# A decoder layer on one core: feed-forward product formed by DVE from the up bank, WKV denominators inverted in pairs, ACT's copy of the up bank dropped, and another order in every queue

## The chip, the cores and the metric

One Trainium2 chip, one of its cores. The metric is the device time of the kernel in microseconds; lower is better. Engines are called as in the profile: PE (TensorE), DVE (VectorE), ACT (ScalarE), POOL (GpSimd), SP (SyncE, which here only issues DMAs).

## What is computed

One decoder layer on 16 sequences of 128 tokens with 256 channels, in float32. First comes an attention over the 16 heads of one token (not over tokens), with a rotary turn, then a WKV recurrence along the 128 tokens, then a feed-forward block whose activations and weights are quantised:

```python
def attn(x):                      # per token: 16 heads of 16
    q, k, v = rope(x @ wq.T), rope(x @ wk.T), x @ wv.T
    w = softmax(einsum('bshd,bstd->bsht', q, k) / sqrt(16))
    return einsum('bsht,bstd->bshd', w, v) @ wo.T
def wkv_step(aa, bb, pp, kt, vt): # along the tokens, per channel
    ww = u + kt; q = max(pp, ww); e1 = exp(pp - q); e2 = exp(ww - q)
    y = (e1 * aa + e2 * vt) / (e1 * bb + e2)
    ...                           # aa, bb decay by exp(-exp(time_decay))
def ffn(x):                       # 256 -> 704 -> 256, weights to -1, 0, 1
    h = silu(bitlinear(x, w1)) * bitlinear(x, w2)
    return bitlinear(h, w3)
x = layernorm(x + attn(x))
x = layernorm(x + wkv(k=x, v=ctx))
x = layernorm(x + ffn(x))
```

`bitlinear` scales each token's activations by 127 over their largest absolute value, rounds them, and multiplies by weights rounded to -1, 0 or 1 by the mean of their absolute values.

## The kernel before

A tile is one sequence: 128 tokens by 256 channels, `TILES` = 16. The kernel is a software pipeline written out by hand, without a scheduler. Each engine has its own in-order queue. Each queue is written by a function `step(at)` that `run_steps` (L75) calls for `s` = 0 to 21; `on(at(d), stage)` issues `stage` for tile `s - d`, if there is one. So the list in an engine's `step` is at once its order within a step and the distance between the tiles that it serves: `at(0)` is the youngest tile, `at(6)` the oldest. `once(at(d), ...)` issues a piece for tile 0 alone. The engines are tied together only by semaphores, and each stage names the counts that it waits for, both for its inputs and for the buffers that it overwrites.

The stages of a tile, in the order of the data:

- Attention. PE `project_q`, `project_kv` (L382 to L394), fp32, into the bank `ps_qkv`; DVE `copy_q` and ACT `copy_kv` put them into `qkv_tok`; DVE turns them with 32x32 block transposes (`q_to_dmajor`, `k_to_dmajor`, `turn_v`); PE `block_v` turns v, ACT `copy_v_blocks` copies it. PE `score` (64 small products), DVE `max_quads`, `max_rows`, `max_hi_part`, `max_lo_part` find the row maxima, PE `shift` subtracts them in the banks, ACT `exp_scores` takes the exponentials of two banks. PE `weigh_v` in two halves, DVE `heads_to_tokens`, `recip_sums`, `normalise`; PE `turn_attn`, ACT `copy_attn`, PE `project_out`, DVE `residual(.,0)`.
- Each of the three layernorms: DVE `moments`, `mean_var`; POOL `inv_std` (three small operations); ACT `layernorm`.
- WKV. PE `turn_k`, ACT `exp_k` (four exponentials into `past` and `now`), POOL `weigh_past`, `weigh_now`, DVE `scan` (L930), POOL `add_now` (L715) makes `frac`, which holds the denominators `frac[:, 0]` and the numerators `frac[:, 1]` of all 256 channels; DVE `recip_den` (L938) inverts the denominators, POOL `divide` (L725) multiplies; PE `turn_y`, DVE `residual(.,1)`.
- Feed-forward. DVE `amax_of_x`, `floor_x`, `recip_x`, ACT `scale_x`, POOL `whole_x`, PE `turn_xq`, ACT `copy_xq`. Then twice, for halves of 352 columns: PE `up` (L502) writes the gate half into bank `ps_a` and the up half into bank `ps_b`; ACT `tanh_gate`; DVE `gate_up` (L961); ACT `copy_up` (L625) copies `ps_b` to `up_s`; POOL `hidden` (L741) multiplies. DVE `amax_of_h`, `floor_h`, `recip_h`, `scale_of_h`, ACT `scale_h`, POOL `whole_h`, PE `turn_hq`, ACT `copy_hq`, PE `down`, DVE `residual(.,2)`, the last layernorm and SP `store`.

POOL has no part in anything that lies in PSUM: whatever it multiplies has been copied to SBUF. Once per launch the weights are rounded: DVE `weight_sums` (L1005), PE `sum_weights`, DVE `weight_scales`, ACT `round_weights` (L646), DVE `cut_weights`, POOL `ternary_weights` (L772). These are long instructions, and they stand in the queues of the first steps.

The waits that the change touches read before:

```python
# PE up(k, half)
wait(pe, up_copied[1], k.t)          # half 0
wait(pe, gate_done[0], k.t + 1)      # half 1
wait(pe, up_copied[0], k.t + 1)
# POOL hidden(k, half)
wait(pool, up_copied[half], k.t + 1)
wait(pool, gate_done[half], k.t + 1)
wait(pool, h_scaled, k.t)
```

## Time and profile before

| | us |
|---|---|
| three runs | 263.08, 262.02, 260.38 |
| median | 262.02 |
| profiled execution | 262.2 |
| its span, first to last instruction | 260.4 |
| PE busy | 208.2 (80%) |
| DVE busy | 217.7 (84%) |
| ACT busy | 160.9 (62%) |
| POOL busy | 161.5 (62%) |

The profile is of one execution. The span is what its rows cover; 1.8 us of the time lie around it. The core has three phases: a fill to about 57 us in which the pipeline is not full and the weights are prepared, a steady stretch to about 201 us, and a tail in which it runs empty. Times in the timeline count from the span's start. An instruction's duration there and the distance to the next start differ a little, since the end of one overlaps the start of the next.

### The profile page before, as it was taken

How to read it: one execution, taken by the hardware profiler on the slowest of the kernel's cores; microseconds unless marked ns; L12 is line 12 of the kernel's file. 1: busy time of each engine (PE TensorE's matmuls, PEld its weight loads, DVE VectorE, ACT ScalarE, POOL GpSimd, SP SyncE). 2: the span in 40 equal slices, each digit the busy share in tenths (PEclk: the TensorE clock that was granted, in tenths of full speed). 3: DMA queues.
4: the chain of work that ended last, by engine and by line, in shares of the span. 5: the costliest groups of instructions: out<-in, count | busy, mean ns of one | idle time of the engine just before them, and what ended most of it. 6: DMA issues, size and time to landing. Idle time of an engine off the chain costs nothing.

```text
span 260.4 us, 9989 instructions
## 1 busy us (share of the span) xinstructions
PE 208.2 (80%) x3778; PEld 139.9 (54%) x3778; DVE 217.7 (84%) x544; ACT 160.9 (62%) x329; POOL 161.5 (62%) x336
## 2 busy tenths in 40 slices
PE   1759699989899999999999999999997795625611
PEld 0235457657666666666666666766665662413310
DVE  2534987999999999999999999999999977686331
ACT  2212175446686877777777787777777665655631
POOL 0100007647866869696968778787777787876541
PEclk9986869999999999999999999999999757555665
DMA  6920002102020020212201120203020201000001
GB/s 194 369 66 23 3 1 65 58 7 64 4 64 3 3 83 23 65 29 58 61 26 43 44 71 17 84 3 83 5 63 3 63 3 40 10 13 21 0 20 42
DMA packets 11968, 12.34 MB, mean 47 GB/s; under 512 B 1872, under 2 KB 11152, under 8 KB 11920
## 3 DMA queue, kind: packets, MB, share of 16 engines
q1 hardware_dynamic: 11200, 11.67, 14.5%
q8 instruction: 30, 0.49, 0.8%
q14 instruction: 18, 0.15, 0.2%
q10 hardware_dynamic: 720, 0.03, 0.2%
HBM read 9.60 MB, written 2.10 MB: 45 GB/s over the span
## 4 chain that ended last, share of the span: by engine, by line
PE 50%; DVE 22%; issue 18%; ACT 4%; POOL 3%; DMA 1%; DVEq 1%; POOLq 0%; ACTq 0%
PE ps_qkv L393 13%; PE ps_s L429 9%; PE ps_o L476 5%; PE ps_w L379 4%; DVE amax_h L972 4%; PE ps_c L528 4%; DVE vT L863 3%; PE ps_a L514 3%; DVE qkD L858 3%; PE ps_b L514 3%; DVE gate L965 2%; DVE den_rec L941 2%; PE ps_o L379 2%; DVE wsum L1009 2%; PE ps_o L462 2%
## 5 line engine op out<-in xcount | busy, mean ns | idle before, releaser
L393 PE MATMUL ps_qkv<-wqkv,xT 128*128 128x512 f32 x64 | 35.5, 683 | 1.9 <-DVE qkv_tok L842 1.9
L733 POOL TENSOR_TENSOR var_eps<-mv,eps 128x1 f32<-128x1 f32 x48 | 9.2, 192 | 39.8 <-DVE mv L925 39.3
L745 POOL TENSOR_TENSOR hid<-gate,up_s 128x352 f32<-128x352 f32 x32 | 29.8, 932 | 2.1 <-ACT up_s L628 1.8
L736 POOL TENSOR_TENSOR rstd<-var_eps,minus_half 128x1 f32<-128x1 f32 x48 | 26.4, 551 | 3.8
L941 DVE RECIPROCAL den_rec<-frac 128x256 f32<-128x256 f32 x16 | 27.7, 1733 | 0.0
L429 PE MATMUL ps_s<-qkD 20*64 20x64 f32 x1024 | 23.9, 234 | 3.3 <-PE ps_s L429 3.3
L462 PE MATMUL ps_o<-probs,v_blk 64*32 64x64 f32 x1024 | 21.7, 225 | 4.6 <-DVE res L908 3.6
L577 ACT ACTIVATE qkv_tok<-ps_qkv 128x512 f32<-128x512 f32 x16 | 9.6, 598 | 25.3 <-PE ps_qkv L393 25.3
L387 PE MATMUL ps_qkv<-wqkv,xT 128*128 128x256 f32 x64 | 19.8, 431 | 6.1 <-DMA wqkv<-wqkv_in 5.3
L429 PEld LDWEIGHTS ps_s<-qkD 20*64 20x64 f32 x1024 | 19.8, 143 | 8.1 <-PE ps_s L429 5.1
L660 ACT ACTIVATE hqT<-ps_c 128x768 bf16<-128x768 bf16 x16 | 13.0, 811 | 16.4 <-PE ps_c L521 16.4
L462 PEld LDWEIGHTS ps_o<-probs,v_blk 64*32 64x32 f32 x1024 | 16.4, 110 | 12.0 <-DVE res L908 6.2
L588 ACT ACTIVATE probs<-ps_s 128x512 f32<-128x512 f32 x32 | 17.8, 599 | 7.8 <-PE ps_s L444 7.7
L644 ACT ACTIVATE x<-res,nmr,rstd 128x256 f32<-128x256 f32 x32 | 19.1, 597 | 4.9 <-POOL nmr L738 1.9
L869 DVE TRANSPOSE_TENSOR_REDUCE quad_max<-ps_s 128x32 f32<-128x1024 f32 x16 | 19.8, 1236 | 1.9 <-PE ps_s L429 1.9
L965 DVE SCALAR_TENSOR_TENSOR gate<-th,ps_a 128x352 f32<-128x352 f32 x32 | 16.0, 499 | 6.3 <-ACT th L623 6.2
L444 PEld LDWEIGHTS ps_s<-neg_eye,max_hi 128*64 128x64 bf16 x512 | 17.7, 115 | 6.6 <-issue 5.4
L623 ACT ACTIVATE th<-ps_a,half_gate 128x352 f32<-128x352 f32 x32 | 17.5, 548 | 5.6 <-PE ps_b L514 4.9
L721 POOL TENSOR_TENSOR frac<-state,now 128x512 f32<-128x512 f32 x16 | 19.0, 1185 | 1.5 <-DVE state L935 1.5
L935 DVE TENSOR_TENSOR_SCAN state<-w_tab,past 128x516 f32<-128x516 f32 x16 | 19.7, 1233 | 0.0
L920 DVE BATCH_NORM_STATS2 stats<-res 128x6 f32<-128x256 f32 x48 | 19.4, 405 | 0.2
L444 PE MATMUL ps_s<-neg_eye,max_hi 128*64 128x64 bf16 x512 | 19.5, 200 | 0.1
(110 smaller groups left out, 569.5 us busy)
## 6 DMA issues: line engine op xcount, KB each, us to landing
xT<-xT_in SPq DMA_DIRECT2D x16, 128.0 KB, 2.4
x_res<-x_in SPq DMA_DIRECT2D x16, 128.0 KB, 2.7
ctxT<-ctxT_in SPq DMA_DIRECT2D x16, 128.0 KB, 2.4
out<-y_out SPq DMA_DIRECT2D x16, 128.0 KB, 1.7
w_raw<-w_in SPq DMA_DIRECT2D x2, 704.0 KB, 6.7
wqkv<-wqkv_in SPq DMA_DIRECT2D x2, 384.0 KB, 4.2
w_raw<-w_in SPq DMA_DIRECT2D x1, 640.0 KB, 8.6
wo<-wo_in SPq DMA_DIRECT2D x1, 256.0 KB, 4.9
```

Source lines behind the costliest of these rows:

```text
L387: last = mm(ps_q, xT[k.slot][:, h, :], wqkv[:, h, 0:C], start=h == 0, stop=h == 1)
L393: last = mm(ps_kv, xT[k.slot][:, h, :], wqkv[:, h, C:3 * C], start=h == 0, stop=h == 1)
L429: last = mm(ps_s[64 * half:64 * half + 64, g % 2, col:col + BLK], kk, q, start=(g < 2 and b < 2), stop=False, skip_group_check=True)
L444: last = mm(o, m, neg_eye[:, half, :], start=False, stop=part is max_lo, skip_group_check=True)
L462: last = mm(ps_o[PAD * g:PAD * g + PAD, dst:dst + BLK], v_blk[k.slot][rows, jj, g, :], probs[rows, g % 2, src:src + BLK], start=True, stop ...
L736: g.tensor_tensor(rstd[i][:], var_eps[i][:], minus_half[:], ALU.pow).then_inc(rstd_done[i], 1)
L745: g.tensor_tensor(hid[:, half * FH:(half + 1) * FH], gate[half][:], up_s[half][:], ALU.mult).then_inc(hid_done[half], 1)
L869: v.tensor_reduce(quad_max[:].rearrange("p s c -> p (s c)"), ps_s[:].rearrange("p b (c x) -> p (b c) x", x=PAD), AX.X, ALU.max, apply_tran ...
L920: v.bn_stats(stats[i][:], res[i][:]).then_inc(stats_done[i], 1)
L935: v.tensor_tensor_scan(flat(state), flat(w_tab), flat(past), 0.0, ALU.mult, ALU.add).then_inc(scanned, 1)
L941: v.reciprocal(den_rec[:], frac[:, 0]).then_inc(den_recips, 1)
L965: v.scalar_tensor_tensor(gate[half][:], th[half][:], 1.0, ps_a[:, 0:FH], ALU.add, ALU.mult).then_inc(gate_done[half], 1)
```

## The change

The reciprocals are taken in pairs: for two neighbouring tokens with denominators a and b, the kernel inverts a x b and multiplies each numerator by the other denominator and by that one reciprocal. POOL forms the pair products (`pair_dens`) and the cross products (`cross_terms`) and, in `divide`, multiplies by the reciprocal, which is read twice by a step of 0. DVE's `recip_den` then has 128x128 elements instead of 128x256. `U_CUT`, the bound on the exponents' offsets, goes from 60 to 50, so that a product of two denominators stays in range. The feed-forward product `hidden` moves from POOL to DVE and reads `ps_b` in PSUM itself; ACT's `copy_up` and the buffers `up_s` are gone. All queues are written in another order, with other distances between the tiles.

```diff
-U_CUT = 60.0
+U_CUT = 50.0
...
-        den_rec = sb("den_rec", [P, HALVES, P])
+        den_pair = sb("den_pair", [P, HALVES, P // 2])
+        cross = sb("cross", [P, HALVES, P])
+        den_rec = sb("den_rec", [P, HALVES, P // 2])
...
             def up(k, half):
...
-                    wait(pe, up_copied[1], k.t)
+                    wait(pe, hid_done[1], k.t)
                 else:
                     wait(pe, gate_done[0], k.t + 1)
-                    wait(pe, up_copied[0], k.t + 1)
+                    wait(pe, hid_done[0], k.t + 1)
...
-            def copy_up(k, half):
-                wait(act, up_done[half], k.t + 1)
-                wait(act, hid_done[half], k.t)
-                fn(up_s[half][:], ps_b[:, 0:FH], ACT.Copy).then_inc(up_copied[half], 1)
...
             def add_now(k):
...
-                wait(pool, den_recips, k.t)
-                wait(pool, y_ready, k.t)
+                wait(pool, pairs_done, k.t)
+                wait(pool, crossed, k.t)
...
+            even, odd = slice(0, P, 2), slice(1, P, 2)
+            def pair_dens(k):
+                wait(pool, frac_done, k.t + 1)
+                wait(pool, den_recips, k.t)
+                g.tensor_tensor(den_pair[:], frac[:, 0, :, even], frac[:, 0, :, odd], ALU.mult).then_inc(pairs_done, 1)
+            def cross_terms(k):
+                wait(pool, frac_done, k.t + 1)
+                wait(pool, y_ready, k.t)
+                g.tensor_tensor(cross[:, :, even], frac[:, 1, :, even], frac[:, 0, :, odd], ALU.mult)
+                g.tensor_tensor(cross[:, :, odd], frac[:, 1, :, odd], frac[:, 0, :, even], ALU.mult).then_inc(crossed, 1)
             def divide(k):
-                wait(pool, frac_done, k.t + 1)
+                wait(pool, crossed, k.t + 1)
                 wait(pool, den_recips, k.t + 1)
                 wait(pool, y_turned, k.t)
-                g.tensor_tensor(yT[:], frac[:, 1], den_rec[:], ALU.mult).then_inc(y_ready, 1)
+                g.tensor_tensor(yT[:].rearrange("p h (n l) -> p (h n) l", l=2),
+                                cross[:].rearrange("p h (n l) -> p (h n) l", l=2),
+                                den_rec[:].rearrange("p h n -> p (h n)").unsqueeze(2).broadcast_to([P, C // 2, 2]),
+                                ALU.mult).then_inc(y_ready, 1)
...
-            def hidden(k, half):                        # on POOL
-                wait(pool, up_copied[half], k.t + 1)
-                wait(pool, gate_done[half], k.t + 1)
-                wait(pool, h_scaled, k.t)
-                g.tensor_tensor(hid[:, half * FH:(half + 1) * FH], gate[half][:], up_s[half][:], ALU.mult
-                                ).then_inc(hid_done[half], 1)
...
             def recip_den(k):
-                wait(dve, frac_done, k.t + 1)
+                wait(dve, pairs_done, k.t + 1)
                 wait(dve, y_ready, k.t)
-                v.reciprocal(den_rec[:], frac[:, 0]).then_inc(den_recips, 1)
+                v.reciprocal(den_rec[:], den_pair[:]).then_inc(den_recips, 1)
...
+            def hidden(k, half):                        # on DVE
+                wait(dve, gate_done[half], k.t + 1)
+                wait(dve, h_scaled, k.t)
+                v.tensor_tensor(hid[:, half * FH:(half + 1) * FH], gate[half][:], ps_b[:, 0:FH], ALU.mult
+                                ).then_inc(hid_done[half], 1)
```

The lists in the five `step` functions are new as a whole. SP issues `load_x`, `load_ctx`, `store` and the feed-forward weights, in this order, as `at(1)`, `at(0)`, `at(5)` and once `at(1)`, where it had the store at 6, the weights at 0, x at 0 and the context at 1. PE's step now begins with `block_v` and `project_out` and ends with `down`; DVE's begins with `residual(.,0)` and ends with `residual(.,2)`, `hidden(.,1)`. For example, of DVE:

```diff
-                on(at(1), max_quads)
+                on(at(0), max_quads)
-                on(at(3), scan)
+                on(at(2), scan)
-                on(at(6), residual, 2)
+                on(at(5), residual, 2)
```

DVE in the steady stretch, from `scale_of_h` (L989, s_h) on. The names are `mv` and `stats` for the layernorms, `den_rec` the reciprocal, `qkD` and `o_tok` transposes, `gate` the product of tanh and gate bank. Before:

```order
L989 TENSOR_SCALAR s_h<-rec_h,s_h 128x1
L925 BN_AGGR mv<-stats 128x2
L941 RECIPROCAL den_rec<-frac 128x256
L858 STREAM_TRANSPOSE qkD<-qkv_tok 128x16x16x2
L965 SCALAR_TENSOR_TENSOR gate<-th,ps_a 128x352
L920 BN_STATS stats<-res 128x6
L890 STREAM_TRANSPOSE o_tok<-ps_o 128x512
L925 BN_AGGR mv<-stats 128x2
L911 TENSOR_TENSOR res<-ps_w,x_0 128x256
L895 RECIPROCAL o_rec<-o_tok 128x16
L920 BN_STATS stats<-res 128x6
L996 TENSOR_SCALAR s_out<-c_h,k_down 128x1
```

The same engine after, also from `scale_of_h` (now L1001); `hid` is the feed-forward product:

```order
L1001 TENSOR_SCALAR s_h<-rec_h,s_h 128x1
L925 BN_STATS stats<-res 128x6
L868 STREAM_TRANSPOSE vT<-qkv_tok 128x16x16x2
L930 BN_AGGR mv<-stats 128x2
L895 STREAM_TRANSPOSE o_tok<-ps_o 128x512
L970 SCALAR_TENSOR_TENSOR gate<-th,ps_a 128x352
L900 RECIPROCAL o_rec<-o_tok 128x16
L977 TENSOR_TENSOR hid<-gate,ps_b 128x352
L905 TENSOR_TENSOR attn<-o_tok,o_rec 128x256
L874 TENSOR_REDUCE quad_max<-ps_s 128x32
L1008 TENSOR_SCALAR s_out<-c_h,k_down 128x1
L881 TENSOR_REDUCE row_max<-quad_max 128x16
```

The reciprocal of the denominators now stands further ahead in the step, the first gate product is followed two places later by `hid`, and the second gate product is the next row behind those shown.

DVE in the fill, around the weight sums (`wsum`) and scales (`wmean`, `wrec`, `k_gate`). Before:

```order
L863 STREAM_TRANSPOSE vT<-qkv_tok 128x16x16x2
L858 STREAM_TRANSPOSE qkD<-qkv_tok 128x16x16x2
L1009 TENSOR_REDUCE wsum<-w_raw 128x1 x3
L890 STREAM_TRANSPOSE o_tok<-ps_o 128x512
L1019 TENSOR_SCALAR wmean<-ps_a 128x3
L1022 RECIPROCAL wrec<-wmean 128x3
L1024 TENSOR_SCALAR k_gate<-wmean 128x1
```

DVE in the fill, after:

```order
L913 TENSOR_TENSOR res<-ps_o,x_res 128x256
L925 BN_STATS stats<-res 128x6
L847 TENSOR_TENSOR qkv_tok<-ps_qkv,turn_gain 128x16x16
L930 BN_AGGR mv<-stats 128x2
L1021 TENSOR_REDUCE wsum<-w_raw 128x1 x3
L858 STREAM_TRANSPOSE qkD<-qkv_tok 128x16x16x2
L863 STREAM_TRANSPOSE qkD<-qkv_tok 128x16x16x2
```

The sums moved behind tile 0's first residual and tile 2's `copy_q`, and the scales to the end of that step. On ACT the rounding (`w_raw`) moved accordingly; before it stood between `copy_v_blocks` and `copy_attn` (`attnT`):

```order
L583 ACTIVATE v_blk<-ps_qkv 128x512
L650 ACTIVATE w_raw<-w_raw,magic,wrec 128x2x704 x2
L650 ACTIVATE w_raw<-w_raw,magic,wrec 128x1536
L593 ACTIVATE attnT<-ps_o 128x256
L577 ACTIVATE qkv_tok<-ps_qkv 128x32x16
```

ACT after, at the same place of the preparation:

```order
L585 ACTIVATE v_blk<-ps_qkv 128x512
L647 ACTIVATE w_raw<-w_raw,magic,wrec 128x2x704 x2
L647 ACTIVATE w_raw<-w_raw,magic,wrec 128x1536
L590 ACTIVATE probs<-ps_s 128x512 x2
L579 ACTIVATE qkv_tok<-ps_qkv 128x32x16
```

It now stands ahead of the exponentials (`probs`) of tile 2 and of `copy_kv` (`qkv_tok`) of tile 3.

## Rows read from the trace of the kernel before

**Rows 1.** The page, chain that ended last, share of the span by engine.
```profile
PE 50%; DVE 22%; issue 18%; ACT 4%; POOL 3%; DMA 1%; DVEq 1%; POOLq 0%; ACTq 0%
```

**Rows 2.** Busy time by stretch; last columns are PE's granted clock, DMA share, GB/s.
```profile
142.66:155.02 12.36, 11.58 (x237) 8.13 (x237) 12.33 (x34) 9.53 (x20) 9.63 (x21) 1.00 0.19 56
...
204.80:217.00 12.20, 10.06 (x157) 7.28 (x157) 8.98 (x22) 8.40 (x18) 9.69 (x20) 0.58 0.09 27
...
229.00:241.00 12.00, 5.58 (x24) 2.92 (x24) 9.34 (x22) 6.27 (x11) 8.26 (x18) 0.50 0.04 12
```

**Rows 3.** Groups of instructions by shape: busy us, mean ns, idle before, releasers.
```profile
L745 POOL TENSOR_TENSOR hid<-gate,up_s 128x352 f32<-128x352 f32 x32 | 29.8, 932 | 2.1 <-ACT up_s L628 1.8 <-DVE gate L965 0.2
L941 DVE RECIPROCAL den_rec<-frac 128x256 f32<-128x256 f32 x16 | 27.7, 1733 | 0.0
...
L721 POOL TENSOR_TENSOR frac<-state,now 128x512 f32<-128x512 f32 x16 | 19.0, 1185 | 1.5 <-DVE state L935 1.5
...
L965 DVE SCALAR_TENSOR_TENSOR gate<-th,ps_a 128x352 f32<-128x352 f32 x32 | 16.0, 499 | 6.3 <-ACT th L623 6.2
...
L713 POOL TENSOR_TENSOR now<-now,ctxT 128x256 f32<-128x256 f32 x16 | 11.6, 728 | 0.0
...
L900 DVE TENSOR_TENSOR attn<-o_tok,o_rec 128x256 f32<-128x256 f32 x16 | 7.6, 475 | 0.1
...
L908 DVE TENSOR_TENSOR res<-ps_o,x_res 128x256 f32<-128x256 f32 x16 | 6.5, 404 | 0.0
...
L895 DVE RECIPROCAL o_rec<-o_tok 128x16 f32<-128x16 f32 x16 | 3.9, 241 | 0.0
```

**Rows 4.** Timeline of DVE in a steady step: start us, us, what.
```profile
146.54 1.73 DVE L941 RECIPROCAL den_rec<-frac 128x256 f32<-128x256 f32 x1
148.19 0.65 DVE L858 STREAM_TRANSPOSE qkD<-qkv_tok 128x512 f32<-128x512 f32 x1
148.77 0.48 DVE L965 SCALAR_TENSOR_TENSOR gate<-th,ps_a 128x352 f32<-128x352 f32 x1
149.17 0.41 DVE L920 BATCH_NORM_STATS2 stats<-res 128x6 f32<-128x256 f32 x1
```

**Rows 5.** Timeline of ACT in the same step.
```profile
146.55 0.97 ACT L655 ACTIVATE hq<-hid,magic,s_h 128x704 f32<-128x704 f32 x1
147.43 0.54 ACT L623 ACTIVATE th<-ps_a,half_gate 128x352 f32<-128x352 f32 x1
147.87 0.45 ACT L628 ACTIVATE up_s<-ps_b 128x352 f32<-128x352 f32 x1
149.36 0.81 ACT L660 ACTIVATE hqT<-ps_c 128x768 bf16<-128x768 bf16 x1 [1.04 <-PE ps_c L521]
150.07 0.59 ACT L644 ACTIVATE x<-res,nmr,rstd 128x256 f32<-128x256 f32 x1
150.57 0.56 ACT L623 ACTIVATE th<-ps_a,half_gate 128x352 f32<-128x352 f32 x1
...
152.14 0.61 ACT L604 ACTIVATE past<-ps_w,u_past 128x128 f32<-128x128 f32 x2
152.64 0.62 ACT L604 ACTIVATE now<-ps_w,u_now 128x128 f32<-128x128 f32 x2
```

**Rows 6.** Timeline of DVE in the fill.
```profile
26.00 4.76 DVE L1009 TENSOR_REDUCE wsum<-w_raw 128x1 f32<-128x1408 f32 x3
...
43.03 1.37 DVE L900 TENSOR_TENSOR attn<-o_tok,o_rec 128x256 f32<-128x256 f32 x1
...
54.31 0.39 DVE L842 TENSOR_TENSOR qkv_tok<-ps_qkv,turn_gain 128x256 f32<-128x256 f32 x1
```

**Rows 7.** Timeline of ACT in the fill.
```profile
31.85 4.57 ACT L650 ACTIVATE w_raw<-w_raw,magic,wrec 128x1408 f32<-128x1408 f32 x3 [5.02 <-DVE k_gate L1024]
```

**Rows 8.** Timeline of DVE in the tail.
```profile
219.36 0.41 DVE L908 TENSOR_TENSOR res<-ps_o,x_res 128x256 f32<-128x256 f32 x1
...
248.39 0.89 DVE L972 TENSOR_REDUCE amax_h<-hid 128x1 f32<-128x704 f32 x1 [0.15 <-POOL hid L745]
```

More of the change, by code:

```diff
@@ L185, in decoder_layer @@
         gate = [sb(f"gate{i}", [P, FH]) for i in range(2)]
-        up_s = [sb(f"up_s{i}", [P, FH]) for i in range(2)]
         hid = sb("hid", [P, HIDDEN])
@@ L301, in decoder_layer @@
         gate_done = [sem(f"gate_done{i}") for i in range(2)]
-        up_copied = [sem(f"up_copied{i}") for i in range(2)]
         hid_done = [sem(f"hid_done{i}") for i in range(2)]
@@ L1026, in step @@
             def step(at):
-                once(at(0), wkv_tables)
-                on(at(4), mean_var, 1)
+                on(at(2), residual, 0)
+                on(at(4), amax_of_x)
+                on(at(2), moments, 0)
                 on(at(0), copy_q)
-                on(at(5), gate_up, 1)
-                on(at(0), q_to_dmajor)
-                on(at(6), residual, 2)
-                on(at(1), max_quads)
-                once(at(2), cut_weights, 0)
-                on(at(4), amax_of_x)
@@ L1036, in step @@
-                on(at(1), max_rows)
-                on(at(4), floor_x)
-                once(at(2), cut_weights, 1)
-                on(at(1), max_hi_part)
-                on(at(4), recip_x)
-                once(at(2), cut_weights, 2)
-                on(at(1), max_lo_part)
-                on(at(3), scan)
-                on(at(0), turn_v)
-                on(at(5), amax_of_h)
-                on(at(2), residual, 0)
-                on(at(5), floor_h)
-                on(at(5), recip_h)
-                on(at(2), moments, 0)
@@ L1050, in step @@
-                on(at(5), scale_of_h)
-                on(at(2), mean_var, 0)
-                on(at(3), recip_den)
-                on(at(0), k_to_dmajor)
-                once(at(1), weight_sums)
-                on(at(4), gate_up, 0)
-                on(at(6), moments, 2)
-                on(at(1), heads_to_tokens)
-                once(at(1), weight_scales)
-                on(at(6), mean_var, 2)
-                on(at(3), residual, 1)
+                on(at(4), floor_x)
+                on(at(3), recip_den)
@@ new lines, in step @@
+                on(at(4), recip_x)
+                on(at(6), moments, 2)
+                once(at(3), cut_weights, 0)
+                on(at(2), mean_var, 0)
+                once(at(2), weight_sums)
+                on(at(5), amax_of_h)
+                once(at(3), cut_weights, 1)
+                on(at(6), mean_var, 2)
+                on(at(5), floor_h)
+                on(at(0), q_to_dmajor)
+                once(at(3), cut_weights, 2)
+                on(at(0), k_to_dmajor)
+                on(at(3), residual, 1)
@@ L1061, in step @@
+                on(at(5), recip_h)
+                on(at(5), scale_of_h)
+                on(at(3), moments, 1)
+                on(at(0), turn_v)
+                on(at(3), mean_var, 1)
+                on(at(1), heads_to_tokens)
+                on(at(4), gate_up, 0)
                 on(at(1), recip_sums)
-                on(at(3), moments, 1)
+                on(at(4), hidden, 0)
+                on(at(1), normalise)
+                on(at(0), max_quads)
                 on(at(5), scale_of_out)
-                on(at(1), normalise)
+                on(at(0), max_rows)
@@ L1066, in _ @@
+                on(at(4), gate_up, 1)
+                on(at(0), max_hi_part)
+                on(at(2), scan)
+                on(at(0), max_lo_part)
+                once(at(2), weight_scales)
+                on(at(5), residual, 2)
+                on(at(4), hidden, 1)
+                once(at(1), wkv_tables)
             run_steps(step)
```

76 lines of the change are left out of this document (38 added, 38 removed).

## The prediction

> **What bounds the kernel now.** Read first the chain that ended last, by engine: PE has half of it and DVE 22%, so neither alone is the answer [rows 1]. Then the busy time by stretch. In the steady stretch one tile passes every 12.36 us; DVE is busy 12.33 us of it and PE 11.58, ACT 9.53, POOL 9.63 [rows 2]. DVE never rests there, so the period is DVE's work; the chain runs through PE only where PE happens to feed DVE in time. In the tail (from about 201 us) DVE is busy 8.98 us of 12.20 and PE's granted clock is 0.58, then 0.50, which is the 1.2 GHz level [rows 2]: there the time is the latency of the last tile's chain. So three questions: what is DVE's work per tile after the change, does the new order keep DVE fed, and what become of fill and tail.
>
> **DVE's work per tile.** The page's durations overlap a little, so I price by the distance from one start to the next. The reciprocal of 128x256 takes 1733 ns, that of 128x16 241 ns [rows 3]: (1733-241)/240 = 6.2 ns per column, so 128x128 is 241 + 112 x 6.2 = 0.94 us, 0.80 less. By distance it is 1.65 us now (146.54 to 148.19) [rows 4] and 0.85 after. Added are two products of 128x352 with one operand in PSUM. No such row exists; the nearest are the gate operation of the same width and also with one operand in PSUM, 499 ns (0.40 by distance, 148.77 to 149.17), and the residual add of 128x256, 404 ns [rows 3, 4]. At the row of its own width one costs 0.41, two 0.82. A product cheaper than the narrower residual add is excluded, dearer than the gate by a tenth is the other end: 0.31 to 0.45, so -0.18 to +0.10 per tile. `recip_h` and `scale_of_h` now stand side by side and the second waits for the first, but `floor_h` and `recip_h` no longer do; that cancels within 0.03. Sum: 12.36 - 0.80 + 0.82 + 0.02 = 12.40 us. The two headline edits cancel on the engine that bounds.
>
> **What the other engines get.** ACT loses two copies of 0.45 us (147.87 is one of them) [rows 5], about 0.9 per tile. POOL loses two products of 932 ns, 1.86 [rows 3], and gains three of 128x128. POOL's two-input rows of 128x512 and 128x256 are 1185 and 728 ns [rows 3], 1.79 ns per column, so 0.50 each by the line and 0.73 at most if the step of two elements costs as much as twice the columns: 1.5 to 2.2. Neither engine bounds; this is worth nothing unless it feeds DVE. On PE, `up(.,1)` waited for the copy of ACT and the gate product; it now waits for gate and then `hidden` on DVE, 0.5 us later. PE has 0.78 us per tile to spare, so that is hidden in the steady stretch, and paid in the tail, twice per tile. In return hidden goes straight to `amax_of_h` on the same engine in 0.5 instead of 0.93 plus a handoff.
>
> **Does the new order keep DVE fed?** I laid the new DVE step out by distances from `residual(.,0)` = 0. The tightest place is from `scale_of_h` (5.42) to the second gate operation (9.84): 4.42 us of DVE work. ACT must do beside it, without a gap, `scale_h` 0.88, tanh 0.44, a layernorm 0.50, the four exponentials 1.00, `copy_hq` 0.71 and the second tanh to its end 0.55, with 0.30 of handoffs: 4.38 us [rows 5]. Slack 0.04. Also tight: `copy_q` to `project_kv` to `copy_kv` to `k_to_dmajor` (3.1 of 3.4 us) and the first gate, 0.0. Everything else has 0.3 or more, `scan` among them (it starts at 10.35, `weigh_now` ends at 10.0). Ready in time, so 12.40, with up to 0.3 more per tile where a handoff is a little longer than I count.
>
> POOL and DVE in each other's way is a cost this trace shows: `normalise`, 475 ns on average [rows 3], took 1.37 us at 43.03 [rows 6], while POOL rounded weights. The Trainium skill, SBUF — State Buffer (Who interferes with whom), says that a DVE instruction with two SBUF inputs and a GpSimd one that reads SBUF exclude each other, the second to issue waiting for all of the first, and that with one SBUF input DVE is not touched; the row agrees. By that page the new `hidden`, which reads PSUM and one SBUF operand, costs nobody anything.
>
> **Fill.** The weight sums hold DVE 4.76 us at 26.00 [rows 6] and PE waits behind them. Now they stand one step later, after `copy_q` of tile 2, where `project_kv` covers some of them. But the rounding, 4.57 us of ACT at 31.85 [rows 7], now stands ahead of both exponentials of tile 2 and `copy_kv` of tile 3. Walking the new order through with the durations of this trace (handoffs 0.05): sums at 31.5 to 36.2, maxima of tile 2 at 42.8, rounding 43.3 to 47.8, `copy_kv` of tile 3 ends 49.4 though its projection stood at 47.3, POOL casts the weights 47.6 to 51.9, which holds the past terms of tile 1 until 53.8, DVE ends step 3 at 55.6. Copy_q of tile 4 is then at 55.6 + 0.94 = 56.5, against 54.31 [rows 6]; but by then the new DVE order has taken also tile 3's row maxima, 1.5 us, which the old had before it. So the fill is worth 0.7 us the wrong way, with 2 us of doubt on either side.
>
> **Steady.** Step 4 lacks the operations of the tiles 5 and 6 behind: 12.40 - 1.69 - 0.43 = 10.28; step 5 is 11.97; steps 6 to 15 are 10 x 12.40 = 124.0. DVE's step 16 starts at 55.6 + 146.25 = 201.9.
>
> **Tail.** Now `residual(15,0)` is at 219.36 and the last `amax_of_h` at 248.39 [rows 8], 12.0 us before the end of the span. Walked with PE at the slow level, the new steps 16 to 19 come to 12.8 (heads of tile 15 wait for a slow `weigh_v`), 12.5, 11.2 and 9.6 us, 46.1 in all: `amax_of_h` of tile 15 at 248.0. `residual(15,0)` comes at 214.7, 4.7 us sooner than before, but this is given back: the new order puts `scan` and `residual(.,2)` between the second gate and `hidden(.,1)`, and `amax_of_x` only behind the whole of the next step, so layernorm 1 of tile 15 is read 7 us after its residual. From there the old 12.0 us stand: amax to `scale_h`, turn, `down`, layernorm, store, of which nothing was changed. Span 260.0.
>
> **Sum.** 260.0 + 1.8 (the profiled execution took 262.2 for a span of 260.4) = 261.8 us. The median of the runs shown is 262.02, so this is no change that can be told: about 1% is what a measurement of this kernel can tell from none.
>
> **Rivals.**
> Faster: the walk is too careful and the shorter pipeline shows. In steady order a tile now needs 6 periods + 8.4 us from its first projection to its last layernorm, before 6 periods + 16.9; 8 us are there to be had. For it: 4.7 us of them did reach `residual(15,0)` in my walk, and the bare chain from there to `amax_of_h`, without any other tile, is about 23 us by adding the mean durations and 0.05 per handoff (an estimate), against the 33 that I let it take. Against: in-order queues hold tile 15 behind tiles 13 and 14 in each step. If all of the 4.7 stays, and 1 us of fill, the time is 256.
>
> Slower: ACT misses the 0.04 us of slack. Every step then waits on DVE for the second tanh; it decides from 0.04 us per step on, and at 0.3 us on 14 steps costs 4.2: 266. For it: there are three places with less than 0.1. Against: before, the old order was as tight by the look of it (DVE idle 0.03 per step) and held.
>
> Slower in another way: POOL runs late. If its three strided products take 0.73 each (0.7 more per tile) and its queue slips by the 0.35 between the end of `weigh_now` and the start of `scan`, then `scan` stands still beside `weigh_now` as `normalise` did in rows 6: up to 0.7 per step on 12 steps, 8.4, so 270. Against: POOL has 2.7 us idle per tile now [rows 2].
>
> That the change does not do what it says: if the reciprocal has a fixed cost that the two rows hide, the saving could be 0.4 rather than 0.8, 5 us slower by 12 steps; the line through 241 and 1733 speaks against it, and I fold it into the slower cases.
>
> **How the numbers follow.** Forecast (between 259.4 and 264.6) 0.42; faster rival 0.32; slower ones 0.26 (ACT's slack 0.16, POOL 0.04, the fill or reciprocal 0.06). Faster by over 1% 0.32, within 0.42, slower by over 1% 0.26. The range leaves out the far tails of both signs: 256.5, just above the full faster rival, to 267.5, above the ACT rival with a little of the fill's doubt. The likeliest case's own range is 259.4 to 264.6.
>
> **What would show it right or wrong.** Right: reciprocal near 0.94 us, `hidden` on DVE near 0.50, DVE busy to within 0.2 us of a period of 12.4; `residual(15,0)` about 4 us earlier than now with the last `amax_of_h` near 248. Step by step wrong: a period over 12.6 with DVE waiting for tanh (ACT) or, at `scan`, for nothing named; POOL products of 0.73; DVE's first gate operation of tile 0 later than about 63 us; a last `amax_of_h` before 245, which would mean that the tail kept its 4.7 us.

## The result, and the profile after

The changed kernel takes 267.26 us (median of 4 runs, 265.40 to 268.76) beside 262.55 us for the kernel before on the same chip: ratio 1.0192, 95% interval 1.0102 to 1.0281. It is 4.7 us slower, and the forecast of 261.8 missed by 5.5. The profiled execution took 267.59 us for a span of 265.6. Here and below, ratios leave out executions in a slower state of the chip and medians in us keep them, so a ratio need not be the quotient of two medians (that of before_warm rests on two executions).

Start with the stretches, as in [rows 2]. The first row below is a full steady step of the changed kernel, the others are its steps 16 to 18 (step 16 from one `residual(.,0)` on DVE to the next, step 17 from there to the maximum of x of tile 14, step 18 from there to that of tile 15). Columns: stretch, length, then busy time (and count) of PE, PEld, DVE, ACT, POOL; granted clock, DMA share, GB/s.

```profile
144.56:156.98 12.42, 11.68 (x237) 7.99 (x236) 12.38 (x36) 8.70 (x19) 9.14 (x22) 1.00 0.16 46
206.67:220.31 13.64, 10.49 (x130) 6.79 (x122) 9.31 (x28) 8.10 (x17) 9.55 (x22) 0.63 0.07 20
220.31:232.60 12.29, 5.71 (x26) 2.92 (x26) 8.26 (x23) 6.34 (x13) 8.94 (x22) 0.72 0.03 11
232.60:243.63 11.03, 5.69 (x24) 2.89 (x24) 6.73 (x19) 4.96 (x8) 5.77 (x16) 0.57 0.05 14
```

The steady step is what was forecast: 12.42 us against 12.36 before, with DVE busy for 12.38 of them. ACT and POOL have been relieved by 0.8 and 0.5 us, and this buys nothing, since DVE is still the engine that never rests. The rows of DVE that carry the two edits answer to [rows 3, 4]:

```profile
149.54 0.38 DVE L916 TENSOR_TENSOR res<-ps_w,x 128x256 f32<-128x256 f32 x1
...
151.77 0.48 DVE L970 SCALAR_TENSOR_TENSOR gate<-th,ps_a 128x352 f32<-128x352 f32 x1
152.18 0.23 DVE L900 RECIPROCAL o_rec<-o_tok 128x16 f32<-128x16 f32 x1
152.34 0.47 DVE L977 TENSOR_TENSOR hid<-gate,ps_b 128x352 f32<-128x352 f32 x1
152.73 0.42 DVE L905 TENSOR_TENSOR attn<-o_tok,o_rec 128x256 f32<-128x256 f32 x1
```

So the loss must lie outside the steady steps. Set the same landmark of both kernels side by side; `amax_of_x` serves, since it is the same stage of the same tile in both (start in us, from the timelines of DVE):

| `amax_of_x` of tile | before | after | difference | what grew |
|---|---|---|---|---|
| 0 | 56.82 | 56.87 | 0.05 | |
| 1 | 67.52 | 69.25 | 1.73 | step 4: 12.38 instead of 10.70 |
| 12 | 203.63 | 207.08 | 3.45 | 11 steps: 1.4 in a clock dip and the step behind it |
| end of span | 260.4 | 265.6 | 5.2 | last tiles: 58.5 instead of 56.8 |

Three places, each worth 1.7 us. The first, step 4, in the timeline of DVE:

```profile
57.53 0.40 DVE L847 TENSOR_TENSOR qkv_tok<-ps_qkv,turn_gain 128x256 f32<-128x256 f32 x1
...
58.31 0.95 DVE L946 RECIPROCAL den_rec<-den_pair 128x128 f32<-128x128 f32 x1 [0.33 <-POOL den_pair L726]
...
61.12 0.71 DVE L863 STREAM_TRANSPOSE qkD<-qkv_tok 128x512 f32<-128x512 f32 x1 [1.16 <-ACT qkv_tok L579]
...
64.76 0.71 DVE L905 TENSOR_TENSOR attn<-o_tok,o_rec 128x256 f32<-128x256 f32 x1
```

Read the brackets: DVE stands 0.33 us for the pair product and 1.16 us for ACT's copy of k and v, which full steps have without a wait. The second place is a dip of the clock at 114 to 118 us. PE is busy throughout it; of the two us ahead of it (112 to 114) it is busy 0.80 and 0.54, of the same two us a step earlier, where no dip follows, 0.80 and 1.00:

```profile
114.00:115.00 1.00, 1.00 (x18) 0.90 (x18) 1.00 (x3) 0.60 (x3) 0.89 (x3) 0.80 0.40 131
115.00:116.00 1.00, 1.00 (x5) 0.52 (x3) 0.95 (x3) 0.81 (x1) 1.00 (x2) 0.50 0.74 213
116.00:117.00 1.00, 1.00 (x6) 0.80 (x5) 0.17 (x1) 0.76 (x2) 0.05 (x1) 0.50 0.15 49
117.00:118.00 1.00, 1.00 (x7) 0.80 (x6) 1.00 (x3) 0.07 (x1) 0.00 (x0) 0.50 0.52 131
```

The granted clock is 0.50, the 1.2 GHz level, for some 3 us, and DVE is busy 0.17 us of the third row, since ACT's second tanh comes late:

```profile
116.83 0.52 DVE L970 SCALAR_TENSOR_TENSOR gate<-th,ps_a 128x352 f32<-128x352 f32 x1 [0.88 <-ACT th L625]
```

The third place is the tail, at that level for most of its length in both kernels.

### The profile page after: what moved, and what is told of

The parts are those of the page before. It is cut to its first block and busy times, and to the rows that moved or that the text cites. A ratio compares the mean times of both kernels' runs of the same rounds, so it can differ in the third digit from the quotient of the medians.

```text
span 265.6 us, 10003 instructions
## 1 busy us (share of the span) xinstructions
PE 212.9 (80%) x3778; PEld 142.2 (54%) x3778; DVE 218.5 (82%) x576; ACT 149.3 (56%) x297; POOL 154.1 (58%) x352
## 5 line engine op out<-in xcount | busy, mean ns | idle before, releaser
L395 PE MATMUL ps_qkv<-wqkv,xT 128*128 128x512 f32 x64 | 33.7, 651 | 4.9 <-DVE qkv_tok L847 4.9
L745 POOL TENSOR_TENSOR var_eps<-mv,eps 128x1 f32<-128x1 f32 x48 | 10.0, 208 | 34.7 <-DVE mv L930 34.6
L431 PEld LDWEIGHTS ps_s<-qkD 20*64 20x64 f32 x1024 | 20.1, 143 | 13.2 <-issue 6.1
L590 ACT ACTIVATE probs<-ps_s 128x512 f32<-128x512 f32 x32 | 18.6, 587 | 14.6 <-PE ps_s L446 14.6
L516 PE MATMUL ps_a<-w,xqT 128*128 128x352 bf16 x64 | 17.6, 362 | 5.1 <-DVE hid L977 3.4
L925 DVE BATCH_NORM_STATS2 stats<-res 128x6 f32<-128x256 f32 x48 | 20.0, 416 | 0.2
L395 PEld LDWEIGHTS ps_qkv<-wqkv,xT 128*128 128x128 f32 x64 | 11.5, 201 | 15.4 <-issue 8.5
L652 ACT ACTIVATE hq<-hid,magic,s_h 128x704 f32<-128x704 f32 x16 | 15.5, 972 | 7.5 <-DVE s_h L1001 7.4
L613 ACT ACTIVATE xq<-x,magic,s_x 128x256 f32<-128x256 f32 x16 | 9.6, 600 | 17.9 <-DVE s_x L964 17.9
```

The source lines that it names most:

```text
L395: last = mm(ps_kv, xT[k.slot][:, h, :], wqkv[:, h, C:3 * C], start=h == 0, stop=h == 1)
L431: last = mm(ps_s[64 * half:64 * half + 64, g % 2, col:col + BLK], kk, q, start=(g < 2 and b < 2), stop=False, skip_group_check=True)
L516: last = mm(bank[:, 0:FH], xqT[:, h, :], w12[:, h, i, cols], start=h == 0, stop=h == 1)
L925: v.bn_stats(stats[i][:], res[i][:]).then_inc(stats_done[i], 1)
```

## The experiments

All ratios are against the kernel before on the chip of that experiment, which took 261.26 to 262.99 us there. The theories are told in the order in which they fell.

### The two parts in the old order

`pairs_old` puts the pair products alone into the kernel before, on POOL right behind `add_now`:

```diff
                 on(at(3), add_now)
+                on(at(3), pair_dens)
+                on(at(3), cross_terms)
                 on(at(4), ffn_scales)
```

> Only the reciprocals in pairs, in the order of the kernel before; the feed-forward product stays on POOL and the copy on ACT. Theory: DVE has 0.80 us less per tile (12.36 to 11.6) and PE, busy 11.6 us with small waits, becomes the bound near 11.8 to 12.0: 12 to 14 steps x 0.4 to 0.6, some 5 to 8 us less, 255 to 257. Rival (the old order was as tight on PE and ACT as on DVE, or POOL with 1.5 us more becomes late): 261 to 263.

`hid_old` puts `hidden` alone on DVE: the second half behind `q_to_dmajor`, the first behind `moments(.,2)`.

> Only the feed-forward product on DVE without ACT's copy, in the order of the kernel before; reciprocals of 128x256. Theory: DVE has 0.82 us more per tile, the period is 13.2 and about 13 steps show it, plus 1 us in the tail: 273 to 276. Rival (DVE's work is hidden elsewhere, by waits that go): below 268.

`both_old` has both, still in the old order.

> Both parts of the arithmetic (reciprocals in pairs on POOL and DVE, feed-forward product on DVE, no copy by ACT) in the order of the kernel before; hidden(.,0) two places behind gate_up(.,0), hidden(.,1) two places behind gate_up(.,1), pair_dens and cross_terms behind add_now. Theory (the new order is what costs): the two parts cancel on DVE, the period stays 12.4 us, the tail grows by about 1 us because hidden now stands between gate and up: 262.5 to 264.5 us. Rival (the arithmetic costs): about 267, as the changed kernel.

`order_only` keeps the old arithmetic and takes the new order: copies of up behind each tanh, `hidden` 0 on POOL behind `whole_h`, `hidden` 1 behind `weigh_now`.

> The old arithmetic (reciprocal of 128x256, copy by ACT, product on POOL) in the new order of all queues; copy_up behind each tanh, hidden(.,0) behind whole_h and hidden(.,1) behind weigh_now on POOL. Theory (the order costs): period 12.4 or a little more, fill and tail as in the changed kernel, 265 to 268. Rival (the arithmetic costs): 262 to 263.5.

Measured: pairs_old 273.08 us, ratio 1.0481 (1.0384 to 1.0579); hid_old 272.01, 1.0442 (1.0359 to 1.0525); both_old 279.04, 1.0713 (1.0592 to 1.0834); order_only 298.89, 1.1473 (1.1389 to 1.1556). Every one is slower than either whole kernel, and pairs_old, from which 0.8 us per tile of the busiest engine was taken, is 4.8% slower. In pairs_old, both_old and order_only the theory and its rival both failed (268 us was the most that either allowed); hid_old came 1 us under its 273 to 276. The steady period of pairs_old is 12.88 us and DVE now waits. The step in both_old, POOL first, then DVE:

```profile
149.62 1.18 POOL L716 TENSOR_TENSOR frac<-state,now 128x512 f32<-128x512 f32 x1
150.88 0.40 POOL L726 TENSOR_TENSOR den_pair<-frac 128x128 f32<-128x128 f32 x1
151.24 0.52 POOL L731 TENSOR_TENSOR cross<-frac 128x128 f32<-128x128 f32 x1
151.72 0.52 POOL L732 TENSOR_TENSOR cross<-frac 128x128 f32<-128x128 f32 x1
...
153.95 0.78 POOL L775 TENSOR_SCALAR hq<-hq 128x704 bf16<-128x704 f32 x1
154.70 0.67 POOL L738 TENSOR_TENSOR yT<-cross,den_rec 128x256 f32<-128x256 f32 x1
```
```profile
155.97 0.42 DVE L916 TENSOR_TENSOR res<-ps_w,x 128x256 f32<-128x256 f32 x1 [0.60 <-PE ps_w L381]
```

The three products stand ahead of all that POOL must do before `whole_h` and `divide`, so both come late, PE turns y late, and `residual(.,1)` waits. In order_only it is the other way round: POOL's long products meet DVE's operations. `hid` took 1.93 us at 143.33 instead of 0.93, while on DVE `max_lo` took 0.83 (144.47) and `attn` 1.15 (154.72); the period is 14.9 us.

`pairs_fix` is pairs_old with `whole_h` and `divide` moved ahead of `inv_std(.,0)` in POOL's list.

> The kernel with the pairs alone in the old order (273.08 us), of which only POOL's list differs: the rounding of the hidden layer and the division stand ahead of inv_std of the first layer norm instead of behind it. Theory (pairs and cross terms on POOL push inv_std 0, and with it rounding and division, 1.1 us later than DVE, so that residual 1 waits 1.1 us per tile): rounding near 152.5 on the old scale, residual 1 loses its wait, the period falls from 12.90 to 12.2 or less, the time to 255 to 262 us. Rival (POOL's own load or PE sets the period, and the late first layer norm only moves the wait to exp_k and the scan): 268 to 274 us, with a new wait on the scan or the first layer norm.

272.65 us, 1.0398 (1.0321 to 1.0475). The theory of the late chain was half right: over the steady stretch DVE waits far less (busy 101.3 of 104.5 us here, 93.8 of 103.0 in pairs_old), but the period is 13.06 all the same, because the waits turned into longer operations:

```profile
155.04 0.80 DVE L923 TENSOR_TENSOR attn<-o_tok,o_rec 128x256 f32<-128x256 f32 x1
```

and the cast of the maxima took 0.65 instead of 0.20 at 146.51. POOL is busy 90.5 of the 104.5 us. The pairs put 1.4 us per tile on POOL, which forms `hidden` too and now works beside DVE for more of the step; `hidden` on DVE alone fills DVE (103.7 of 104.0 us, period 13.2). In the old order the two edits do not make up for each other either (1.0713 together, more than either alone), and the new order with the old arithmetic is the slowest of all. Only all three together come near the kernel before. One edit alone in the new order was not run, so these runs do not give each part a price of its own.

### Once more, and the ends

`after_again` is the changed kernel unaltered.

> The changed kernel unaltered, beside the next three on the same chip. If its loss lies where its first trace shows it (fill, tail), the time is 265 to 269 us again and the profile shows the same landmarks within 0.5 us: amax_x of tile 0 near 56.9, residual 0 of tile 15 near 220, residual 1 of tile 15 near 236, the last amax of the hidden layer near 253.6. If the clock dip of 114 to 118 us was chance, it is gone or elsewhere and the span is up to 1 us shorter; if it belongs to the kernel, it stands at the same place.

266.15 us, 1.0150 (1.0096 to 1.0205). Landmarks as in the first trace within 0.3 us up to tile 4 and the dip at 114 to 118 us again, so it is no chance of one execution. It costs less there (13.10 and 12.65 us for the two steps, after 13.47 and 12.71), and step 16 took 12.80 instead of 13.64, so that the last `amax_of_h` came at 252.16 instead of 253.63. Of the twelve traces of this study that run the new order with the new arithmetic (in half_pool with half of `hidden` on POOL), nine have a steady step lengthened by the low clock (all but tail_new, warm_tail and scale_later); the three of the old kernel and its padded versions have none.

`tail_new` gives x2 a third buffer and, from step 16 on, puts layer norm 1 ahead of the second tanh and the maximum, scales and rounding of x in the same step. `x2_three` has only the buffer.

> The changed kernel; only the steps after the last tile has entered (16 to 21) differ: x2 gets a third buffer, layer norm 1 of the tile three behind stands ahead of the second tanh on ACT, and its maximum, scales and rounding follow in the same step instead of the next. Theory (the tail's order costs about 4 us: maximum of tile 15 at 239.45 before, 243.63 after): the maximum of x of tile 15 comes 3 to 4 us sooner after residual 1 of that tile, and the time falls by 3 to 4.5 us, to 263 to 264. Rival (the last steps are bound by the hidden layer and the down product on PE and DVE anyway, so that a sooner maximum only waits longer): under 1 us, 266 to 267.5.

> The changed kernel with one edit: x2 gets a third buffer, so that layer norm 1 no longer waits for residual 2 of the tile two before. In the run with the rearranged tail (which has this buffer too) the steady period was 12.34 instead of 12.42 us and the clock dip of step 8 was missing. Theory: both come from the buffer (ACT's layer norm 1 stands ahead of the first exponentials, and was held back 0.9 us each tile), the loss without it is 0.08 us in each of 15 steps plus about 1 us for the dip: maximum of x of tile 11 at 192.0 to 193.3 us instead of 194.0 to 194.7, the tail as in the changed kernel, the time 263.5 to 265. Rival (the dip is not tied to the buffer): only the 0.08 per step, dip present at 114 to 118 us, 265 to 266.

tail_new 265.64 us, 1.0139 (1.0087 to 1.0190); x2_three 268.38, 1.0247 (1.0172 to 1.0322). The maximum of tile 15 did come 4.86 us after `residual(15,1)` instead of 7.78, but step 16 was 1.4 us longer (DVE waits 1.27 us for ACT's x at 215.25) and the way from the maximum of x to that of the hidden layer 11.0 instead of 10.0: from `amax_of_x(12)` to the end 58.2 us, as in the changed kernel (58.5, 57.7). The buffer does shorten the period, to 12.34 us, but x2_three has two steps with the low clock (13.25 and 13.03 us, granted 0.87 on average), each with a step of 12.71 behind it, and loses that again; it came out above both the theory and the rival.

`fill_new` moves the weight load a step earlier, the scales behind the first transpose of step 2 and ACT's rounding ahead of its attention copy. `fill_split` takes POOL's ternary weights apart over steps 3 and 4.

> The changed kernel; only the once-only work on the feed-forward weights moves: the load is issued one step sooner, the sum over partitions stands ahead of the third tile's scores on PE, the scales follow the first transpose of step 2 on DVE instead of the end of that step, and ACT rounds the weights ahead of the attention copy of step 2 (about 37 to 41.5 us) instead of at its end (42.48 to 47). Theory (the round stands on the path of step 3, PE idle behind it falls to the low clock, and step 4 pays 2 us): exponentials of the third tile come 3 us sooner, residual 0 of step 4 at 54.5 to 55.5 instead of 56.5, step 4 below 11.8 us, time down by 2 to 3 us, 264 to 265.5. Rival (the fill is set by DVE and by the ternary weights on POOL): same time within 1 us, 266 to 267.5.

> The changed kernel with the rounding to ternary weights on POOL taken apart: w1 stays where it is in step 3, w2 follows behind weigh_now of step 3, w3 (with its cut on DVE) goes to step 4. Theory (in step 3 DVE has no idle time; it loses 3 us to the cuts and about 2 us to operations that wait out POOL's 1.39 us weight operations: attn 1.47 instead of 0.42, scan 1.74 instead of 1.23, cast 0.31 instead of 0.17): residual 0 of step 4 comes 1.5 to 2.5 us sooner than 56.4, step 4 takes 0.9 us more for the third cut, net 0.5 to 1.5 us sooner at residual 0 of step 5 (68.9), time 265 to 266.5. Rival (the collisions only move to other operations, the cut as well): no change within 0.5 us at residual 0 of step 5.

fill_new 268.60 us, 1.0221 (1.0156 to 1.0287), fill_split 267.38, 1.0216 (1.0146 to 1.0285): no gain in either. In fill_new the rounding ran at 37.78, as meant, and from `residual(.,0)` of step 2 to that of step 5 it is 39.9 us, in the changed kernel 39.5. In fill_split step 3 fell from 13.72 to 13.16 us and step 4 rose from 12.39 to 13.14. As far as these two runs show, rounding and collisions fill time that is waited for anyway.

`half_pool` gives the second half of `hidden` back to POOL, into the 1.59 us in which it waits for the scan (with the third x2 buffer).

> The changed kernel with the third x2 buffer and the second half of the hidden layer back on POOL (up values copied by ACT behind the second tanh, the product in the time in which POOL waits for the scan, 1.59 us per tile); the first half stays on DVE, the pairs stay. DVE gives up 0.51 us per tile and has no idle time now. Theory (DVE alone sets the steady period once each wait is covered; PE is next with 11.76 of 12.42): period 11.8 to 12.0 us, time 258 to 261. Rival (the product collides with the scan on DVE, or add_now and with it the pair reciprocal come late): period 12.3 or more, with a wait on the pair product, the scan above 1.5 us, time 264 or more.

270.35 us, 1.0341 (1.0279 to 1.0404), period 12.60. The rival came true, though in another place than it said; the scan itself is not longer:

```profile
143.53 1.87 POOL L765 TENSOR_TENSOR hid<-gate,up_s 128x352 f32<-128x352 f32 x1 [0.38 <-DVE gate L985]
```
```profile
143.44 1.23 DVE L955 TENSOR_TENSOR_SCAN state<-w_tab,past 128x516 f32<-128x516 f32 x1
144.59 0.84 DVE L905 TENSOR_TENSOR max_lo<-row_max,max_hi 128x16 bf16<-128x16 f32 x1
```

POOL's product overlaps the scan and ends 0.7 us after it; then one of DVE's smallest operations, `max_lo`, takes 0.84 instead of 0.15 us. DVE gave up 0.51 and got back 0.69.

### The clock

Five kernels add matmuls that nobody reads (identity by weights, 128x256, into the free bank ps_b) where PE waits.

```diff
+            def warm(n):
+                for _ in range(n):
+                    mm(ps_b[:, 0:C], ident[:], wqkv[:, 0, 0:C], start=True, stop=True)
...
+                once(at(3), warm, 3)
                 on(at(1), weigh_v, 0)
...
+                once(at(2), warm, 4)
                 on(at(0), score)
```

That is `warm_fill`. `warm_tail` has them ahead of `turn_y` in steps 16 to 18 (4, 5, 8), of `turn_xq` in step 19 (6) and of the last `turn_hq` (8). `before_warm` has 22 in the same way in the tail of the kernel before.

> The changed kernel with seven added matmuls of identity by weights into a bank that is free there and that nobody reads: four ahead of the third tile's scores (gap 34.9 to 36.8 us), three ahead of weigh_v of step 3 (gap 47.0 to 48.2 us). Theory (step 4 loses 1.5 us of waits because TensorE runs at the low clock from 50 to 56.8 us, behind the gap): the granted clock stays at the high level from 36 to 57 us, the copy of k and v of step 4 comes in time, step 4 takes 10.6 to 11.2 us instead of 12.39, maximum of x of tile 1 at 66.5 to 68 us instead of 69.1, time down by 1.2 to 2.5 us. Rival (DVE is busy throughout step 3 with cuts and collisions, the clock only fills slack): clock high, but maximum of x of tile 1 at 68.5 us or later, time the same within 0.7 us.

> The changed kernel with 31 added matmuls that nobody reads in TensorE's long gaps of the last steps: ahead of turn_y in steps 16, 17 and 18, ahead of turn_xq in step 19, ahead of turn_hq in step 20. Theory (the tail is a chain through TensorE at the low clock: matmuls of 0.77 instead of 0.46 us and so on, about 2 us per step on the chain): granted clock at the high level for most of 210 to 260 us, residual 1 of tile 15 to the end shorter by 2 to 5 us, time 261.5 to 264.5. Rival (what stands on the chain is DVE, POOL and ACT, or the added matmuls overrun the gaps): within 1 us of the changed kernel, 265 to 268.

> The kernel before with 22 added matmuls that nobody reads in the gaps of its last steps (ahead of turn_xq of tiles 13, 14 and 15 and of the last turn_hq). If the clock sets the tail, it gains 1.5 to 4 us (257.5 to 260) and beats both kernels; if it does not, it is the same as before within 1 us. The changed kernel's tail is worse than before's by its order only if before_warm gains no more than warm_tail does.

warm_fill 266.28 us, 1.0142 (1.0056 to 1.0227); warm_tail 263.07, 1.0032 (0.9993 to 1.0072); before_warm 260.39, 0.9849 (0.9716 to 0.9982). warm_fill missed: the low clock did not go but came later (granted 0.76 from 50 to 54 us and 0.50 from 54 to 58, where the changed kernel has 0.50 from 50 to 56), and step 4 took 13.11 us, 0.7 longer. In the tail of warm_tail the first row is step 16, the second step 17 but for its last 0.8 us, the last runs from the maximum of x of tile 15 on:

```profile
206.93:218.35 11.42, 8.68 (x138) 5.77 (x130) 9.34 (x27) 7.39 (x17) 8.95 (x22) 1.00 0.08 24
218.35:229.90 11.55, 7.54 (x36) 4.30 (x36) 7.86 (x24) 6.04 (x13) 8.65 (x22) 0.85 0.04 13
...
240.96:260.00 19.04, 10.43 (x62) 7.48 (x61) 7.95 (x25) 7.12 (x11) 5.47 (x15) 0.99 0.06 21
```

Step 16 is 11.42 us instead of 13.64 (12.80 in after_again). The added work shortens the time, since the matmuls on the chain run at the high level. `warm_all` closes all these gaps and one more in step 3, `before_warm_all` also the gap of 2.24 us in the fill of the kernel before.

> The changed kernel with the added matmuls of warm_fill and of warm_tail, and two more ahead of the attention transpose of step 3 (gap of 0.91 us at 53 us). Theory (step 4 loses its time to the clock): granted clock at the high level from 36 to 62 us, no wait above 0.5 us at the transpose of k in step 4, residual 0 of step 5 at 67.5 us or sooner counted from residual 0 of step 1 at 30.8 (it was 70.5 in warm_tail), time 258.5 to 261.5. Rival (the low clock only shows the wait; the order of the fill makes the copy late): wait at the transpose of k still above 1 us, time 262 to 264 as warm_tail.

> The kernel before with the added matmuls of before_warm and five more ahead of the sum of the weights (gap of 2.24 us at 30 us in its fill). If the difference between the kernels lay in the clock of fill and tail alone, this kernel and warm_all come within 1 us of each other; if the order of the changed kernel costs something at any clock, this one is 1.5 us or more faster than warm_all. Expected for itself: 258 to 260.5 us, the clock of 30 to 38 us at the high level, up to 1 us gained over before_warm (260.39).

warm_all 263.13 us, 1.0005 (0.9975 to 1.0035); before_warm_all 259.36, 0.9897 (0.9833 to 0.9961). From `amax_of_x(12)` to the end: before 56.8 us, after 58.5 and 57.7; with the clock held up 53.9 and 53.3 for the old kernel, 53.5 and 53.5 for the new. At the high clock the two tails are equal.

The two kernels are not. warm_all and before_warm_all ran on one chip, and the kernel before keeps 3.8 us of advantage: by its own expectation this run says that the changed kernel costs something at any clock. In the traces (spans 259.8 and 255.3) it is 1.4 us up to `amax_of_x` of tile 0, 1.6 in step 4 (12.27 and 10.70), 1.3 in the 11 steps behind it (137.46 and 136.14, one clock dip among those of warm_all) and 0.2 in the tail.

And in warm_all step 4 can be read without the low clock:

```profile
50.00:54.00 4.00, 3.27 (x70) 2.41 (x60) 3.90 (x7) 1.59 (x6) 3.82 (x6) 1.00 0.00 0
54.00:58.00 4.00, 3.25 (x73) 2.55 (x73) 3.64 (x10) 1.40 (x3) 2.76 (x5) 1.00 0.16 40
58.00:62.00 4.00, 3.81 (x58) 1.75 (x60) 3.00 (x7) 2.59 (x6) 3.41 (x10) 1.00 0.22 65
```
```profile
60.61 0.71 DVE L883 STREAM_TRANSPOSE qkD<-qkv_tok 128x512 f32<-128x512 f32 x1 [0.96 <-ACT qkv_tok L599]
```

The wait for k and v is still there, step 4 takes 12.27 us against 12.39: my theory that the clock makes step 4 long had fallen, but for 0.1 to 0.2 us.

### Step 4

The way from `copy_q` over the projection of k and v and ACT's copy to `k_to_dmajor` took 3.6 us in step 4 (57.53 to 61.12). In a full step DVE has 1.35 us of work of the tiles 5 and 6 behind between the two ends; in step 4 there is none. `cover` adds one unused reduction of 704 values there, in step 4 alone; `scale_later` puts `scale_x` behind the copy of k and v in ACT's list of that step.

```diff
                 once(at(2), weight_sums)
+                once(at(4), cover)
                 on(at(5), amax_of_h)
```

> The changed kernel with one more reduction of 704 values on DVE (0.85 us, its result unused) in step 4 alone, at the place where the full steps have amax_h. Theory (the wait at the transpose of k is a chain of fixed length that stage 5 and 6 hide in full steps): the wait of 1.16 us shrinks to 0.3 us and step 4 stays within 0.15 us of 12.39. Rival (DVE's own work sets step 4): 13.1 us or more.

> The changed kernel; in step 4 alone ACT's scale_x stands behind the copy of k and v instead of ahead of it. Theory (chain of fixed length, projection on PE ends just before the copy): the wait at the transpose of k falls by 0.4 us at most and step 4 takes 12.0 us or more. Rival (scale_x holds the copy up): the wait is gone, step 4 at 11.2 to 11.6 us.

```profile
61.31 0.85 DVE L1021 TENSOR_REDUCE cov<-wqkv 128x1 f32<-128x704 f32 x1
62.08 0.70 DVE L859 STREAM_TRANSPOSE qkD<-qkv_tok 128x512 f32<-128x512 f32 x1
63.29 0.71 DVE L864 STREAM_TRANSPOSE qkD<-qkv_tok 128x512 f32<-128x512 f32 x1 [0.51 <-ACT qkv_tok L580]
```

With 0.85 us more on DVE, the wait falls from 1.16 to 0.51 and step 4 takes 12.52 instead of 12.39 us (one execution each, so only the steps are compared, not the times; cover 269.0 us, scale_later 269.85, the kernel before 262.93). In scale_later the wait stays at 1.25, ACT having stood 1.31 us for PE's projection before its copy, and step 4 grows to 15.6 us, because the feed-forward values of tile 0 now come late and what stands behind them in PE's queue with them. Both say the same: it is a chain that DVE's own work neither lengthens nor shortens, and step 4 has nothing to hide it under.

How long the chain is depends a little on PE. The projection of k and v, in the changed kernel and in warm_all:

```profile
58.47 1.98 PE L395 MATMUL ps_qkv<-wqkv,xT 128*128 128x512 f32 x4
```
```profile
57.66 1.98 PE L395 MATMUL ps_qkv<-wqkv,xT 128*128 128x512 f32 x4
```

In the changed kernel it starts 0.94 us after the start of `copy_q` (57.53), because PE, which ran at the low level from 50 to 56.6 us, only then ends `shift`; in a full step (146.09 after 145.63) and in warm_all (after 57.20) it starts 0.46 us after it. From `copy_q` to `k_to_dmajor` it is 3.6 us in the first and 3.4 in warm_all. In the kernel before, the copy of this tile stood at 54.31 [rows 6], so far ahead of the transpose that it never waits:

```profile
62.15 0.65 DVE L858 STREAM_TRANSPOSE qkD<-qkv_tok 128x512 f32<-128x512 f32 x1
```

## Why the prediction missed, step by step

- **DVE's work per tile: right.** Reciprocal 0.94 us forecast, 945 ns measured; `hidden` 0.50, 497 ns; period 12.40, 12.42. "The two headline edits cancel on the engine that bounds" held.
- **Other engines: right in kind.** POOL's products took 0.40 and 0.51 us, at and below the lower end of my 0.50 to 0.73. ACT kept up; the slower rival with ACT's slack did not come true in steady steps.
- **Fill to step 4: 0.9 us short.** Step 4 began at 56.53 instead of 55.6, inside the doubt of 2 us. No run takes this part apart.
- **The step that failed:** "Step 4 lacks the operations of the tiles 5 and 6 behind: 12.40 - 1.69 - 0.43 = 10.28". It took 12.39, 2.1 us more. I took work away from DVE and let the step shrink by it, though I had noted myself that the way from `copy_q` to `k_to_dmajor` needs 3.1 us of 3.4. The missing work was what covered it. Of the 2.1, the waits are 1.49 (0.33 and 1.16), a slowed `attn` is 0.3, and the last 0.3 are gaps of about 0.1 each where the operation that is gone stood between two that depend on each other. The 0.33 is of the same kind as the 1.16: from the end of the scan to `recip_den` DVE has 2.25 us of work in a full step and 1.38 here, while POOL needs 1.7 for the sum and the pair product. The old order loses nothing there: `copy_q` stood 7.8 us ahead of `k_to_dmajor` (54.31 and 62.15), and step 4 took 10.70 without a wait.
- **Steps 6 to 15: 1.6 us short.** 125.57 instead of 124.0, of which 1.05 is the step with the clock dip (13.47) and 0.3 the one after it. I had not thought of a dip in the steady stretch; the trace of before has none.
- **Tail: right but for 0.9.** 46.96 us instead of 46.1, and 11.97 to the end instead of 12.0. The way from `residual(15,0)` to the last `amax_of_h` was forecast at 33.3 us and took 33.32 (29.03 before). But it began at 220.31, not at 214.7, and so 1 us later than before instead of 4.7 sooner: there was no gain to give back. Step 16 alone is 0.8 over. The slow clock, which makes up some 3 to 5 us of the tail (58.5, 57.7 and 56.8 against 53.3 to 53.9), I had read in [rows 2] and treated as given.

The errors are 0.9 + 2.1 + 0.2 (step 5) + 1.6 + 0.9 = 5.7 us, all of one sign, which is the miss. The measured 267.26 lies just inside the widest range that I gave, 256.5 to 267.5, but that is luck: its upper end stood for ACT missing its slack in every step, and in the full steps DVE never waits for ACT. The prediction also took it that a DVE operation with one SBUF input is not held by POOL; the cast of the maxima, which has one, took 0.65 instead of 0.20 us beside POOL's products in pairs_fix, so this does not hold for every operation. `hidden` itself kept to its 0.50 us. Against the kernel before, the 5.2 us of span are step 4 (1.7, shown by cover to be an uncovered chain), the steady stretch (1.7, of it 1.4 the dip and the step behind it; the cause of the dip stays open) and the tail (1.7 and 0.9 in two traces, gone when the clock is held up). So two of the three are shown by runs, and the cause of the one between them is not.

No version of the changed kernel beats the kernel before; the kernel before with padded gaps does, at 0.9849 (0.9716 to 0.9982) and 0.9897 (0.9833 to 0.9961).

## What to carry to other kernels

When a step of a pipeline is short of some of its work, ask for each chain through it what hid the chain in the full step, before you take the work off its length. When two engines are both near full, an edit that frees one by loading the other can be worth nothing alone, however large it looks; try it together with what makes room, and look at the in-order queue behind the added work. And where the clock of TensorE is low in a stretch that is bound by latency, unread matmuls in its waits are a cheap trial: here 31 of them gave 3 us in the tail, while 7 in the fill alone only moved the low clock.

## What the runs showed of the hardware that was not expected

- POOL and DVE slow each other well beyond large operands: beside a POOL product of 128x352, DVE's operation of 128x16 took 0.84 us instead of 0.15 (half_pool), and the product took 1.87 instead of 0.93 beside the scan. It works on one-column operations too: in fill_new, while DVE cut the weights, POOL's add of eps took 0.83 us instead of 0.19.
- POOL's products with a step of two elements, 128x128, took 0.40 us (den_pair) and 0.51 (cross); the line through the rows of 128x256 and 128x512 gave 0.50. No packed product of 128x128 was run, but nothing here shows a price of the step.
- The granted clock fell to the low level in steady steps in which PE was busy (114 to 118 us), at the same place in both traces of the changed kernel, and not at all in others. In warm_all, where the clock came back from its last low stretch of the fill at 43.6 us instead of 56.6, the dip began at 101.6 instead of 114.6, also 13 us sooner and in step 7 instead of 8; so it is not tied to one step of the kernel. No run here shows what starts it.
